# A graph kernel's two weighted neighbour sums, over gathered rows or over a matrix of weights

## The reference, cut to what matters

```python
deg = segment_sum(ones_like(edge_weight), dst, num_segments=n)
inv_deg = where(deg > 0, 1.0 / maximum(deg, 1.0), 0.0)[:, None]
h = relu(layernorm(x))
for l in range(2):
    msg = h[src] * edge_weight[:, None]
    h_neigh = segment_sum(msg, dst, num_segments=n) * inv_deg
    h = h @ W_self[l].T + h_neigh @ W_neigh[l].T + b_neigh[l]
    if l < 1:
        h = relu(h)
x = x + h
```

## Time and profile before

| | us |
|---|---|
| median of the runs | 11507.88 |
| profiled execution | 11493.85 |
| its span | 11492.0 |
| PE busy | 7803.2 (68%) |
| PEld busy | 5533.5 (48%) |
| DVE busy | 7897.7 (69%) |
| ACT busy | 2331.1 (20%) |
| POOL busy | 5213.4 (45%) |

### The profile page before, as it was taken

One profiled execution on the slowest core, in us unless ns is written; L12 is line 12 of the kernel. 1 busy time (PEld: TensorE's weight loads), 2 busy tenths in 40 slices (PEclk: granted clock), 3 DMA queues, 4 the chain that ended last, 5 costly groups with the idle time before them and its releaser, 6 DMA issues. The chain is left out here.

```text
span 11492.0 us, 176718 instructions
## 1 busy us (share of the span) xinstructions
PE 7803.2 (68%) x44549; PEld 5533.5 (48%) x44550; DVE 7897.7 (69%) x11191; ACT 2331.1 (20%) x8740; POOL 5213.4 (45%) x5215
## 2 busy tenths in 40 slices
PE   6888899788878875565477556546745555655557
PEld 4666677566656663333266223226722233522226
DVE  7777555577667776777899677689855556655558
ACT  1222444200000001111187111117800000000000
POOL 3444555344444435777400577740035552155550
PEclk9999999899999997777655667765566777877678
DMA  2333444344444435777588577757923333333333
GB/s 83 91 92 86 113 121 124 94 117 117 113 101 115 117 93 193 243 247 249 150 331 352 189 247 243 244 154 312 374 72 74 75 76 73 110 74 75 75 70 104
DMA packets 812828, 1718.89 MB, mean 150 GB/s; under 512 B 365243, under 2 KB 447176, under 8 KB 757202
## 3 DMA queue, kind: packets, MB, share of 16 engines
q1 hardware_dynamic: 440902, 1154.81, 28.7%
q0 software_dynamic: 193584, 397.91, 16.4%
q10 hardware_dynamic: 178256, 165.14, 4.3%
HBM read 1273.09 MB, written 444.21 MB: 149 GB/s over the span
## 5 line engine op out<-in xcount | busy, mean ns | idle before, releaser
L693 PE MATMUL ps_G<-table_parts,low_onehots 125*128 125x320 bf16 x21840 | 3373.4, 314 | 531.4 <-issue 248.4
L528 POOL DMA_INDIRECT gathered_rows<-node_table,index x2080 | 1981.0, 952 | 2205.0 <-PE ps_sum L548 1477.3
L693 PEld LDWEIGHTS ps_G<-table_parts,low_onehots 125*128 125x128 bf16 x21840 | 2181.8, 102 | 1571.9 <-issue 319.5
L528 POOL DMA_INDIRECT gathered_rows<-xl_table,index x1664 | 1836.2, 1103 | 1579.4 <-PEq L1498 931.8
L528 POOL DMA_INDIRECT gathered_rows<-rel_table,index x1456 | 1386.5, 952 | 2142.0 <-ACT index L518 1165.8
L1510 PE MATMUL ps_Z<-xr,onehots_wide 125*128 x3328 | 1443.6, 590 | 1070.8 <-issue 603.9
L548 PE MATMUL ps_sum<-messages,onehots 128*125 128x65 f32 (+3 forms) x13312 | 1949.6, 310 | 242.7 <-DVE messages L1907 181.8
L548 PEld LDWEIGHTS ps_sum<-messages,onehots 128*125 128x125 f32 x13312 | 1877.9, 226 | 317.8 <-issue 302.9
L723 DVE TENSOR_TENSOR rows_by_feature<-ps_G,fifth_onehots 128x320 f32<-128x320 f32 x1456 | 706.7, 485 | 1638.6 <-remote 950.0
L1510 PEld LDWEIGHTS ps_Z<-xr,onehots_wide 125*128 125x128 f32 x3328 | 775.9, 247 | 1738.5 <-issue 1616.0
L1558 DVE TENSOR_TENSOR z<-gathered_rows,ps_Z 128x650 f32<-128x650 f32 x832 | 661.5, 825 | 694.1 <-issue 409.9
(11 more groups left out here) (328 smaller groups left out, 7044.8 us busy)
## 6 DMA issues: line engine op xcount, KB each, us to landing
stash_a<-gathered_rows SPq DMA_DIRECT2D x208, 1300.0 KB
kept_rows<-stash_a SPq DMA_DIRECT2D x208, 1300.0 KB
onehots<-onehots_kept SPq DMA_DIRECT2D x520, 500.0 KB
onehots_turned<-onehots_turned SPq DMA_DIRECT2D x416, 250.0 KB
low_rows<-low_rows SPq DMA_DIRECT2D x416, 187.5 KB
stash_r<-gathered_rows ACTq DMA_DIRECT2D x208, 272.0 KB
kept_rows<-stash_r SPq DMA_DIRECT2D x208, 272.0 KB
onehots_kept<-onehots ACTq DMA_DIRECT2D x104, 500.0 KB
```

The lines of the kernel that those rows point to most:

```text
L528: pool.indirect_dma_start(G[:, HALF * k + q, 0:width], None, table, bass.IndirectOffsetOnAxis(IDX[:, k, q:q + 1], 0)).then_inc(gathered[k] ...
L693: last = nc.tensor.matmul(ps_G[:, (fetch * k + g) % 2, 0:D * FIVE], OT[0:BN, k, g, a, :], HP[:, part, a, :, :].rearrange("p f b -> p (f b) ...
```

## The change

A new step, matrix_phase, makes one dense matrix of the weights by source and destination in DRAM, `matrix`: 3125 rows (source) of 3168 float32 (destination; rows are padded), 39.6 MB. Then each of the two passes is a product of this matrix with H (matrix_sums).

*Zeroing.* At the start of the setup VectorE clears a tile and ScalarE issues 25 writes of it to 125 rows of the matrix each, and one to 34 spare rows. SP writes two new fields of the edges, a key (source times 3168 plus destination) and the weight, to DRAM (`key_rows`).

*The matrix pass.* For each group SP loads the keys and weights of its eight chunks to all 128 partitions. VectorE compares, for each edge, the keys of its chunk with its own, multiplies the result with the weights and with "stands in front of it", and sums both up: a weight sum of all edges with the same key, and whether it is the first of them. The first one has the place key, all others a spare place. GpSimd issues eight indirect DMAs per group that add 128 values of four bytes each to their places in the matrix. The destination one-hots, the counts by source and now by destination, the stored one-hots and the turned ones are all made in this pass as well. GpSimd waits for the zeroing, and in front of each group for the landing of the group two before. Chunks that follow each other (a strand of 26) are scattered in different turns, so that two scatters in flight don't add to the same place; the first destination of each strand goes to an extra column of its own (32 of them), which a last product adds to the sums.

*The two products.* SP loads the matrix in 25 blocks of 125 rows by 3157 columns, four tiles in turn; TensorE multiplies each with the block's 125 x 64 rows of H, one product for each of the 25 destination blocks and one for the extra columns, adding up in PSUM. The gathers, lookups, messages and the table writes of this layer are gone.

The diff at its core:

```diff
+WIDTH = 3168
+EACH = NCH // (K * HALF)
+STRANDS = K * HALF
+COLS = N + STRANDS
@@ setup, SP @@
-                    write_rows(sp)
+                    for a, rows_of in enumerate((pair_key[:, :, :], fields[:, 3, :, :])):
+                        sp.dma_start(key_rows.rearrange("(t p) a c -> p t a c", p=P)[:, :, a, :], rows_of).then_inc(s_lowD, 16)
@@ setup, ScalarE, ahead of everything else @@
+                    act.wait_ge(s_cnt, 1)
+                    for b in range(NB):
+                        act.dma_start(matrix[BN * b * WIDTH:BN * (b + 1) * WIDTH, :].rearrange("(p w) o -> p (w o)", p=BN),
+                                      blank[0:BN, :]).then_inc(s_zeroD, 16)
+                    act.dma_start(matrix[N * WIDTH:(N + SPARE) * WIDTH, :].rearrange("(p w) o -> p (w o)", p=SPARE),
+                                  blank[0:SPARE, :]).then_inc(s_zeroD, 16)
@@ setup, VectorE @@
+                    v.memset(blank[:, :], 0.0).then_inc(s_cnt, 1)
...
+                    v.scalar_tensor_tensor(pair_key[:, :, :], a_src, float(WIDTH), a_dst, ALU.mult, ALU.add).then_inc(s_over, 1)
@@ matrix_phase, SP @@
+                        def load_keys(i, k):
+                            sp.dma_start(KW[:, k, :, :, :].rearrange("p q a c -> p q (a c)"),
+                                         rows_of[bass.ds(i, 1), k, :, :].rearrange("o q x -> (o q) x").partition_broadcast(P)).then_inc(keys_in[k].sem, 16)
@@ matrix_phase, GpSimd @@
+                        pool.wait_ge(s_zeroD, 16 * (NB + 1))
...
+                                if not (first_turn and k < K // 2):
+                                    landed = scattered[(k + K // 2) % K]
+                                    pool.wait_ge(landed.sem, landed.at(16 * HALF * (i + k // (K // 2))))
+                                pool.sem_inc(places_free.sem, 1)
+                                pool.wait_ge(index_made.sem, index_made.at(K * i + k + 1))
...
+                                for q in range(HALF):
+                                    pool.indirect_dma_start(matrix, bass.IndirectOffsetOnAxis(PL[:, k, q:q + 1], 0), RS[:, k, 0, q:q + 1], None,
+                                                            compute_op=ALU.add).then_inc(scattered[k].sem, 16)
@@ matrix_phase, VectorE, per group @@
+                            v.tensor_tensor(EQ[:, :, :], KW[:, k, :, 0, :], of_group(mine, i, k).to_broadcast([P, HALF, C]), ALU.is_equal).then_inc(key_steps.sem, 1)
...
+                            v.tensor_tensor(TW[:, 0, :, :], EQ[:, :, :], KW[:, k, :, 1, :], ALU.mult).then_inc(key_steps.sem, 1)
...
+                            v.tensor_tensor(TW[:, 1, :, :], EQ[:, :, :], before_it[:, :].unsqueeze(1).to_broadcast([P, HALF, C]), ALU.mult).then_inc(key_steps.sem, 1)
...
+                            v.tensor_reduce(RS[:, k, :, :], TW[:, :, :, :], AX, ALU.add).then_inc(key_steps.sem, 1)
...
+                                one_hot(Lo, low_all, i, k, BN)
...
+                                one_hot(Hi, high_all, i, k, NB)
...
+                                one_hot(HD, block_f, i, k, NB)
...
+                                one_hot(S, dloc, i, k, BN).then_inc(onehot_made.sem, 1)
@@ matrix_phase, TensorE, per group @@
+                                    last = nc.tensor.transpose(ps_T[0:BN, k % 2, q, :], SN[:, HALF * k + q, :], ident_b[:, :])
...
+                                    nc.tensor.matmul(ps_hist[0:BN, 0:NB], Lo[:, j, :], Hi[:, j, :], start=False, stop=True, skip_group_check=True)
+                                    last = nc.tensor.matmul(ps_hist[0:BN, P:P + NB], SN[:, j, :], HD[:, j, :], start=False, stop=True, skip_group_check=True)
@@ matrix_sums @@
+                            if b >= RING:
+                                sp.wait_ge(blocks_multiplied.sem, blocks_multiplied.at(b - RING + 1))
+                            sp.dma_start(MR[:, b % RING, :], matrix[BN * b * WIDTH:BN * (b + 1) * WIDTH, :].rearrange("(p w) o -> p (w o)", p=BN)[:, 0:COLS]
+                                         ).then_inc(loaded[b % RING].sem, 16)
...
+                            for d in range(NB):
+                                sum_chunk(ps_sum, MR[:, b % RING, :].rearrange("p (o w) -> p o w", o=1)[:, :, BN * d:BN * (d + 1)], 0, H[:, b, :], D, D * d)
+                            nc.tensor.matmul(ps_sum[0:STRANDS, NB * D:(NB + 1) * D], MR[:, b % RING, N:COLS], H[:, b, :],
+                                             start=False, stop=True, skip_group_check=True).then_inc(blocks_multiplied.sem, 1)
...
+                        for d in range(NB):
+                            last = nc.tensor.matmul(ps_sum[0:BN, D * d:D * (d + 1)], heads[:, BN * d:BN * (d + 1)], tail[:, :],
+                                                    start=False, stop=True, skip_group_check=True)
@@ the layer @@
+            matrix_phase(heads, inv_deg, has)
             for l in range(2):
-                weighted_sums(CAT, inv_deg, has, l == 0)
+                matrix_sums(CAT, inv_deg, heads)
```

More of the change, by code:

```diff
@@ L735, in picks_over, with matrix_phase @@
             table_split.over(1)
-        def weighted_sums(CAT, inv_deg, has, hist):
+        EQUAL, WEIGHED, RANKED, SUMMED, FIRST = range(1, 6)
+        STEPS = 5
+        def matrix_phase(heads, inv_deg, has):
             phase[0] += 1
@@ L770, in _ @@
                     def _(sp):
[L771 to L777 removed]
+                        rows_of = key_rows[0:NCH, :, :].rearrange("(q k i) a c -> i k q (a c)", k=K, i=EACH)
@@ L812, in _ @@
-                                last.then_inc(msg_made.sem, 1)
-                                keep_index(act, IDX, src_all, i + 1, k)
+                                if not (last_turn and k == K - 1):
+                                    narrow(i, k + 1)
+                                act.wait_ge(turned.sem, turned.at(n + 1))
+                                act.wait_ge(turned_out[k].sem, turned_out[k].at(16 * i))
+                                nc.scalar.activation(ST[0:BN, group_of(k), :], ps_T[0:BN, k % 2, :, :], ACT.Copy).then_inc(turned_copied.sem, 1)
@@ new lines, in turn @@
+                                n = K * i + k
+                                more = not (last_turn and k >= K - 2)
+                                if more:
+                                    dve.wait_ge(key_steps.sem, key_steps.at(STEPS * (n + 1) + SUMMED))
+                                    compare(i, k + 2)
+                                chunks_free(dve, i, k)
+                                one_hot(Lo, low_all, i, k, BN)
+                                if more:
+                                    weights(i, k + 2)
@@ L844, in _ @@
                         turn(TURNS - 1, True)
[L845 removed]
+                        dve.wait_ge(ramps, 3)
+                        link(v.tensor_scalar(heads[:, :], nodes, head[:, 0:1], None, ALU.is_equal))
                         dve.wait_ge(finished, 1)
[L847 to L848 removed]
@@ L858, in _ @@
-                        for some, ps in banks:
-                            last = v.tensor_tensor(CAT[:, some, D:2 * D], ps[:, :, 0:D],
-                                                   inv_deg[:, some].unsqueeze(2).to_broadcast([BN, ps.shape[1], D]), ALU.mult)
-                        link(last)
+                        link(v.tensor_copy(deg_out[:, :], ps_hist[0:BN, 0:NB]))
+                        link(v.tensor_copy(deg_in[:, :], ps_hist[0:BN, P:P + NB]))
+                        link(v.tensor_scalar(has[:, :], deg_in[:, :], 0.0, None, ALU.is_gt))
@@ L880, in turn @@
-                                if not hist:
-                                    pe.wait_ge(narrow_made.sem, narrow_made.at(n + 1))
-                                    pe.wait_ge(turned_copied.sem, turned_copied.at(n))
-                                    for q in range(HALF):
-                                        last = nc.tensor.transpose(ps_T[0:BN, q, :], SN[:, HALF * k + q, :], ident_b[:, :])
-                                    last.then_inc(turned.sem, 1)
-                                if not (last_turn and k == K - 1):
-                                    fetch_rows(pe, OT, HP, ps_G, i, k + 1)
@@ L1068, in build @@
                 if l == 0:
-                    dense(CAT[:, :, :], 2 * D, [w0[:, l, :]], take, None, None, write_rows, between)
-                    rows_over()
+                    dense(CAT[:, :, :], 2 * D, [w0[:, l, :]], take, None, last_of)
                 else:
                     dense(CAT[:, :, :], 2 * D, [w0[:, l, :]], take, None, after)
+        zs.close()
         ls = ExitStack()
@@ L1843, in shared_sums @@
                 ps_sum = pb("ps_sum", [P, 7 * BANK], F32, es)
-                ready, finished = (once(x) for x in ("set_up", "loop_over"))
                 with nc.Block() as block:
```

380 lines of the change are left out of this document (226 added, 154 removed).

## The result

The changed kernel takes 12,039.9 us (median of 4 runs, 11,964.8 to 12,146.5), the kernel before 11,505.8 in the same measurement. The ratio is 1.046, with a 95% interval of 1.043 to 1.049: slower. One of the four runs (12,146.5, granted clock 0.692 instead of 0.70) was in a slower state, and the ratio leaves it out. I had forecast 11,475 and a range of 11,410 to 11,800.

The account below looks back on a forecast made before the run. It took GpSimd's scatters to pace the matrix pass and loads the products: pass end 1422 + 324 + 20 + 324 + 18 = 2108 us against 2143, 35 less, so 11,475 us; range 11,410 to 11,800.

Parts of the forecast that it names:

- The scatters: Matrix pass: GpSimd sets the pace with 832 scatters at a gather's 1.25 us start to start, 1038 us.
- Rival A: Matrix pass, slower: adding scatters cost more, or the low engines lag; at 1.60 us each 11,766; gain gone at 1.29; chance 0.36.
- My own upper bound: Matrix pass: 2.0 us per scatter, from slow starts of the same kind of instruction, 1664 us for 832.
- The gather's row: Profile row for gathers, used to price a scatter: 0.94 us busy, the next starts 1.25 us after it.
- VectorE: Matrix pass: its work takes 8.8 us a group, below GpSimd's 10.0, so it does not set the pace.
- Zeroing and setup: Start of the kernel: zeroing over at about 315 us, setup ends at 358 instead of 87, costing 271 more.
- Five engines: Zeroing and matrix loads: transfers 125 rows high use 5 of 16 DMA engines, taken at 131 GB/s.
- that sign: Setup: X lands between 240 and 310 us, so norm's first reduction comes after 240.
- the three paths: Ends of the setup: from X 286 to 356 us, from ScalarE's root 317, from SP's issues 358; 358 taken.
- Rival B: Setup, faster: X or the weights aren't delayed, first scatter at 335, 42 us less, 11,433; chance 0.13.
- rival C: Zeroing and matrix loads, much faster: new transfers use all 16 engines, 487 us less, 11,020; chance 0.06.
- The products: Two layers after the matrix pass: each limited by its loads, 12.0 us a block, 324 us a layer.

Follow-up runs that it names:

- plain: The changed kernel with its 832 scatters writing their value instead of adding it: 11,643.6 us.
- plainport: As plain, against which the tile of equal keys moves from SBUF to PSUM: 11,650.6 us.
- rows64: The changed kernel with each adding scatter naming 64 partitions instead of 128, half of the pairs left out: 11,857.5 us.
- half: The changed kernel with only the first four of each group's eight scatters issued: 11,282.7 us.
- wide: The changed kernel with zeroing in transfers of 128 rows and each block loaded as 112 + 13 rows: 11,675.7 us, ratio 1.026.

## Why the prediction was wrong

- **The scatters: the step that failed.** The term was 832 x 1.25 us, put at 1038 (it is 1040), "I take 1.25, the row that the same instruction has for nearly all of its run". Measured: 1.85 us start to start, 1.91 in the mean, 1592 us. Of the 550 missing in the pass, 487 are the price of adding (832 x 0.585, `plain`), 51 VectorE's two-input products (`plainport` shows the mechanism; the size is mean less median), 7 landings. GpSimd set the pace as forecast; the price of its instruction was mis-sized. The other stages miss by less than 10 us each.
- **The range.** Rival A had the mechanism, the break-even (1.29 us) and the sign, and a price of 1.60 with no row behind it. My own upper bound was 2.0 us, 1664 for the pass. The range ended at 1.64, left out the upper half of that bound, and the measured 1.91 lies in it. With a rate of 83 us for each tenth, the range had to reach 12,100.
- **Why the row misled.** The gather's row is a row of the same instruction and not of the same work: "the gather's time does not follow the bytes" says nothing on what an added operation costs. Part of the extra goes by rows (`rows64`: 0.13 us for 64 rows), the larger part is paid once an instruction by the estimate there.
- **VectorE.** Forecast 8.8 us a group, 9.18 measured (`half`); below GpSimd's pace in both cases, so its own pace cost nothing. That its operations with two SBUF inputs lengthen GpSimd's scatters was in no step.
- **Zeroing and setup: right.** Five engines, 134 GB/s, ScalarE free at 283 (275), matrix block at 349 (358), first scatter 370 (377). X landed at 219 where I had 240 to 310, so that sign was missed. It cost nothing: of the three paths SP's ended last, as forecast, with its last issue at 342.7. Rival B (X near 40 us) is out; rival C too, since 125 rows did not use 16 engines, and `wide` shows that it was the number of rows.
- **The products: right, 683 against 686 us.** TensorE at half clock needs 10.8 us a block (11.7 forecast), the loads come 11.8 apart (12.0 forecast); they are a near tie, which is why `wide` gained only 42 us on both layers.
- **What was expected to be saved.** The passes did lose their 2010 us. They came back as 283 of setup, 1604 of scatters and their ends, and 643 of products; the dense steps are 7 shorter.

## What to carry to other kernels

When a change swaps an instruction for a variant of it that no row shows, and hundreds stand in a row on one engine, let the range reach the end of the bound, or make the choice of the variant the main rival with its full price. Look at the height of every transfer first: zeroing in 128 rows instead of 125 moved 422 GB/s instead of 134, and loads of 112 + 13 rows 200 instead of 123, for an edit of a few lines. A conclusion from two runs needs them on one chip, with the kernel before beside them.

## What the runs showed of the hardware

- An indirect scatter that adds occupies GpSimd for 1.54 us, one that writes for 0.96, a gather for 0.94; 64 rows instead of 128 take 0.13 us off one that adds. On GpSimd's queue a scatter of 128 values is 144 packets when it adds and 32 when it writes.
- A plain scatter took 0.87 us longer while VectorE multiplied two SBUF tiles, and nothing longer while it reduced one; with one operand of the products in PSUM the mean extra falls from 0.20 to 0.05 us.
- With all scatters into cells that lie side by side and an eighth of the keys, GpSimd waits 440 us (adding) and 604 (writing) for landings, in a pass that has 7 and 74 otherwise. That the places are the cause is not shown.
- With products of 64 moving columns and a new 125 x 125 load each time the granted clock was 0.51 (near 1.2 GHz), with TensorE busy for 91% of the layer; with the same sums in products of up to 512 moving columns it was 0.94 (near 2.4 GHz), with TensorE busy for 82%.
- Reads of the matrix in 112 + 13 rows reach 200 GB/s at a share of 0.84, in 125 rows 123 GB/s at 0.29: for each engine's busy time the wide reads move about half as much. Why was not tried.
- One program takes 11,506 us on one chip, about 11,370 on three and 10,337 on two. In the profiles of the last two kinds the busy times agree within 2%, and TensorE's waits for issue (1150 and 78 us) make up the difference. Their cause is open.
